# The stage ahead of the exponentials: two token buffers, key tiles ahead of query tiles, scores over 51 rows, fewer clearings, waits by chunk

## The chip, the cores and the metric

The kernel runs on one core of one Trainium2 chip. The metric is the device time of one execution in microseconds (us). Of the kernel before there are three timed runs and one profiled execution. Engines are named as in the profile: PE (TensorE matmul), PEld (TensorE weight load), DVE (VectorE), ACT (ScalarE), POOL (GpSimd), SP (SyncE, which issues nearly all DMAs).

## The reference, cut to what matters

Four samples of 2048 tokens with 256 features pass an adaptive layer norm, a differential attention and a ternary linear layer:

```python
h = _layernorm(x) * (1 + ca) + sa
q, k = h @ Wq.T, h @ Wk.T                 # 32 score heads of 8 features
v = h @ Wv.T                              # 16 value heads of 16 features
scores = (q * 8 ** -0.5) @ k.T            # 2048 x 2048 for each score head
attn_w = softmax(scores)                  # float32
aw = attn_w[:, :, 0] - lam * attn_w[:, :, 1]
attn = rmsnorm(aw @ v) * subln_w * (1 - LAMBDA_INIT)
x = x + ga * (attn @ Wo.T)
h = _layernorm(x) * (1 + cb) + sb
x = x + gb * (h @ (ternary(weight) * scale).T)
```

## The kernel before, in words

A sample (B = 4) has NC = 4 chunks of CH = 512 tokens, and a chunk has 4 blocks of 128 tokens. The program has two parts.

**The first part** works on sample 0 alone, chunk by chunk (`tc`), before any exponential. For one chunk:

- SP loads 512 tokens (512 KB) into `a_x` (`a_load`).
- DVE takes mean and variance (`a_stats`), POOL raises the variance to the power -1/2 (`a_power`), DVE writes `normed` (`a_apply`, L1103).
- PE transposes `normed` (`turn`, L831, 64 PE instructions), ACT copies the result to `p_hT` with the modulation's scale and bias (`turned`, L760).
- PE projects four tiles of 128 features: 0 and 1 are the queries, 2 and 3 the keys (L845, 64 instructions for two tiles), then the values (L837, 64 instructions). The order on PE is: projections of `tc`, `turn(tc + 1)`, values of `tc`.
- ACT copies each tile out of PSUM to `a_qk` (`projected`, L770 and L772) and its bf16 head to `p_parts` (L776). POOL subtracts (`rest`, L707), ACT rounds again (`middle`, L781), POOL subtracts again (`low`, L713). A float32 number thus becomes three bf16 parts. `p_parts` has two buffers, one of which lies in `probs`.
- DVE takes signs and absolute maxima of query tiles (L1146, L1147) and maximum and minimum of key tiles (L1148, L1149) in `first_bounds`, and copies the values to `a_v` (`first_values`, L1165).
- SP stores the parts to scratch in DRAM (`store_qk`, L447, three DMAs for one tile) and the values (`store_v`, L451), and reads back what group 0 needs (`first_rows`, L486 and L493, five DMAs; it waits until the chunk's parts and values have landed).

After the last chunk an upper bound of each query's scores is formed from the extremes of all keys. DVE builds `box_w` (`m_means`), PE multiplies it with the signed queries in six steps (`m_step`, L895), DVE reduces these (`m_evacuate`, L1310 and L1311), splits the result in three bf16 parts (`maxima_split`, L1327 to L1331), PE transposes them (L882), ACT copies them to `m_parts` (L797), and SP writes them from there into three rows of `queries[0]` (`first_maxima`, L518, four DMAs of 2048 tokens). The keys have ones in the same three rows (written by `clear(keys[i], ONE_PAIR)`), so that the score product subtracts the bound by itself.

**The second part** is the attention. `queries` and `keys` hold two halves, at rows 0 and 64. A half has KQ = 48 rows of products of parts and 3 rows of maxima. A score product reads KS_ROWS = 64 rows of a half; the 13 rows that remain are zero in `queries` (cleared by POOL at the start). For 128 keys and 512 queries of one pair, PE makes two score products (`scores`, L915), ACT takes one exponential over 1024 columns (L810), and PE multiplies with the values (`weighted`, L932). Two exponentials make a unit; a body has 128 units and the program 16 bodies. Pieces of the next sample's first part and of the last sample's output part lie between the units by a written table (`steps_of`). PE waits for all loads of a group (`group_loaded`, `loads_of`) before the first unit of that group. SP, PE and DVE wait for `m_flag`, which says whether the bound is too loose; in the profiled execution the branch behind it is not taken.

The order on each engine is that of the code; no planner or scheduler is at work. Waits are on counting semaphores.

## Time and profile before

| | us |
|---|---|
| median of 3 runs | 3849.46 |
| lowest and highest | 3845.53, 3850.63 |
| profiled execution, its own time | 3844.91 |
| profiled execution, span | 3843.2 |

| engine | busy us | share of the span |
|---|---|---|
| PE | 3685.4 | 96% |
| ACT | 3712.2 | 97% |
| DVE | 2149.8 | 56% |
| POOL | 623.0 | 16% |

The busy time of an engine is a mean over two parts with different limits. In the first of 40 slices of the span (96 us each) ACT is busy for 3 tenths, in each of the 38 slices that follow for 9 tenths or more, and in the last for 4. A busy PE is not PE at its peak, since ends of matmuls are modelled. The granted clock of PE is a mean over a stretch of two levels, 1.2 GHz (0.50) and 2.4 GHz (1.00).

### The profile page before, as it was taken

What the parts mean: (1) busy time and instruction counts of PE and PEld (TensorE: products, weight loads), DVE (VectorE), ACT (ScalarE), POOL (GpSimd) and SP (SyncE); (2) the same over time, 40 slices, a digit from 0 to 9 for tenths busy, and PEclk for the clock granted to TensorE, in tenths of its full rate; (3) what the DMA queues carried; (4) which work ended last, traced back from release to release, by engine and by line L of the source; (5) the groups of instructions that cost most, each with busy time, mean ns of one, the idle gap of its engine ahead of it and who ended that gap; (6) DMA issues with size and microseconds to landing.
All of it is one profiled execution on the core that took longest, in us unless ns stands there. A gap on an engine that the chain in (4) does not pass through costs nothing.

```text
span 3843.2 us, 76108 instructions
## 1 busy us (share of the span) xinstructions
PE 3685.4 (96%) x32110; PEld 933.9 (24%) x32110; DVE 2149.8 (56%) x3654; ACT 3712.2 (97%) x4067; POOL 623.0 (16%) x402
## 2 busy tenths in 40 slices
PE   7999999999999999999999999999999999999997
PEld 5222222122222222222222222222222222211122
DVE  7556656463366666665347566666435566555233
ACT  3999999999999999999999999999999999999994
POOL 5111212112121211212112121211211111010010
PEclk8999999999999999999999999999999999999998
DMA  7221121212212221131121212221112111201101
GB/s 242 53 67 26 47 43 39 50 34 56 49 42 48 59 53 42 47 68 39 46 53 52 57 36 48 61 51 43 46 35 51 31 42 31 46 4 25 37 20 41
DMA packets 132420, 188.33 MB, mean 49 GB/s; under 512 B 11100, under 2 KB 107100, under 8 KB 132064
## 3 DMA queue, kind: packets, MB, share of 16 engines
q1 hardware_dynamic: 131248, 182.53, 19.3%
q8 instruction: 257, 4.21, 0.5%
q14 instruction: 99, 0.81, 0.1%
q10 hardware_dynamic: 816, 0.79, 0.1%
HBM read 97.61 MB, written 85.47 MB: 48 GB/s over the span
## 4 chain that ended last, share of the span: by engine, by line
ACT 54%; PE 29%; issue 13%; DVE 2%; SPq 1%; POOL 0%; DMA 0%; DVEq 0%; ACTq 0%; POOLq 0%
ACT probs L810 52%; PE ps L932 15%; PE ps L915 10%; PE ps L837 2%; ACT wmod_sb L810 2%; DVE seg_t L1255 1%; PE ps L845 1%; PE ps L831 1%; DVE normed L1103 0%; SPq L447 0%; PE ps L895 0%; DMA v_scr<-a_v 0%; SPq L486 0%; DMA a_x<-in_x_dram 0%; DVE e_tmp L1207 0%
## 5 line engine op out<-in xcount | busy, mean ns | idle before, releaser
L810 ACT ACTIVATE probs<-ps 128x1024 f32<-128x1024 f32 x3894 | 3584.0, 1206 | 22.1 <-PE ps L915 21.2
L932 PE MATMUL ps<-probs,values 128*32 128x512 f32 x15576 | 2077.1, 605 | 7.7 <-DVE seg_t L1255 3.0
L915 PE MATMUL ps<-queries,keys 64*128 64x512 bf16 x8192 | 1395.6, 385 | 89.5 <-DMA queries<-wmod_sb 7.0
L915 PEld LDWEIGHTS ps<-queries,keys 64*128 64x128 bf16 x8192 | 347.3, 93 | 1727.8 <-ACT probs L810 1560.8
L743 POOL TENSOR_TENSOR seg_rs<-seg_ms,neg_half 64x16 f32<-64x16 f32 x128 | 370.2, 2892 | 2372.7 <-DVE seg_ms L1264 2372.7
L1255 DVE STREAM_TRANSPOSE seg_t<-ps 128x512 f32<-128x512 f32 x128 | 91.8, 717 | 1001.2 <-PE ps L932 1001.2
L932 PEld LDWEIGHTS ps<-probs,values 128*32 128x32 f32 x15576 | 306.9, 108 | 593.8 <-issue 489.9
L1243 DVE SCALAR_TENSOR_TENSOR wmod_sb<-wmod_sb,d_y 128x1024 f32<-128x1024 f32 x303 | 371.1, 1225 | 10.4
L1229 DVE TENSOR_SCALAR d_y<-ps 128x1024 f32<-128x1024 f32 x101 | 123.7, 1225 | 124.3 <-PE ps L915 124.3
L810 ACT ACTIVATE wmod_sb<-ps 128x1024 f32<-128x1024 f32 x101 | 129.8, 1285 | 0.0
L831 PE MATMUL ps<-ident,normed 128*32 128x128 f32 x2048 | 103.8, 295 | 25.7 <-DVE normed L1103 25.7
L1244 DVE SCALAR_TENSOR_TENSOR wmod_sb<-wmod_sb,gates 128x1024 f32<-128x1024 f32 x101 | 123.7, 1225 | 3.5
L1241 DVE SCALAR_TENSOR_TENSOR wmod_sb<-d_y 128x1024 f32<-128x1024 f32 x101 | 123.1, 1219 | 0.0
L1239 DVE TENSOR_TENSOR d_y<-d_y,gates 128x1024 f32<-128x1024 f32 x101 | 119.7, 1185 | 0.8
L1273 DVE SCALAR_TENSOR_TENSOR seg_a<-seg_n,subln_sb 32x256 f32<-32x256 f32 x256 | 109.3, 427 | 6.0
L1207 DVE TENSOR_TENSOR e_tmp<-ps,e_gate 128x512 f32<-128x512 f32 x64 | 44.2, 691 | 120.3 <-PE ps L837 120.3
L831 PEld LDWEIGHTS ps<-ident,normed 128*32 128x32 f32 x2048 | 71.5, 120 | 153.2 <-issue 138.2
L932 PE MATMUL ps<-wmod_sb,values 128*32 128x512 f32 x808 | 107.6, 605 | 0.0
L683 POOL CAST a_parts<-a_qk 128x512 bf16<-128x512 f32 x48 | 29.4, 613 | 411.8 <-DVE wmod_sb L1244 396.8
L1269 DVE TENSOR_TENSOR seg_n<-seg_d,seg_rs 64x256 f32<-64x256 f32 x128 | 54.6, 426 | 68.0 <-POOL seg_rs L743 64.5
L1277 DVE STREAM_TRANSPOSE seg_o<-seg_a 32x512 f32<-32x512 f32 x128 | 89.6, 700 | 4.4
L837 PE MATMUL ps<-w_f,e_hT 128*32 128x256 f32 x1024 | 80.0, 397 | 8.3 <-DVE e_hT L1204 6.6
(153 smaller groups left out, 1733.6 us busy)
## 6 DMA issues: line engine op xcount, KB each, us to landing
queries<-q_scr SPq DMA_DIRECT2D x62, 384.0 KB
keys<-k_scr SPq DMA_DIRECT2D x62, 384.0 KB
v_scr<-a_v SPq DMA_DIRECT2D x16, 1024.0 KB, 4.5
values<-v_scr SPq DMA_DIRECT2D x31, 512.0 KB
q_scr<-a_parts SPq DMA_DIRECT2D x28, 384.0 KB, 2.6
k_scr<-a_parts SPq DMA_DIRECT2D x28, 384.0 KB, 2.6
a_x<-in_x_dram SPq DMA_DIRECT2D x16, 512.0 KB, 12.8
attn_scr<-seg_o SPq DMA_DIRECT2D x128, 64.0 KB, 1.7
```

The costliest lines, as they stand in the source:

```text
L743: nc.gpsimd.tensor_tensor(seg_rs[:, :], seg_ms[:, :], neg_half[0:64, :], ALU.pow).then_inc(seg_rs_done, 1)
L810: nc.scalar.activation(probs_of(unit)[:, n % PAIRS, :, :], slots[slot_of(body, n)], ACT.Exp).then_inc(exp_done, 1)
L831: last = nc.tensor.matmul(bank[j:j + 32, n * P:(n + 1) * P], src[:, n, c * P + j:c * P + j + 32], ident[:, :], start=True, stop=True)
L837: last = nc.tensor.matmul(bank[j:j + 32, (n % 2) * E:(n % 2 + 1) * E], hT[:, c, n * P + j:n * P + j + 32], w[:, c, :], start=(c == 0), sto ...
L915: last = nc.tensor.matmul(slots[slot_of(body, n)][:, half, :], keys[buf][at:at + KS_ROWS, n % PAIRS, blk * P:(blk + 1) * P], queries[buf][ ...
L932: last = nc.tensor.matmul(pv[j:j + VW, :], values[buf][:, blk, half, :], probs_of(unit)[:, pair, half, :], start=(blk == 0), stop=(blk == ...
L1229: V.tensor_scalar(d_y[:, :], slots[n % SLOTS].rearrange("p h c -> p (h c)"), EXP_LOW, QUARTER_LOG2E, ALU.max, ALU.mult).then_inc(d_read, 1)
L1239: link.then(V.tensor_tensor(d_y[:, :], d_y[:, :], d_n, ALU.subtract))
L1241: link.then(V.scalar_tensor_tensor(d_out, d_y[:, :], POLY[4], d_y[:, :], ALU.add, ALU.mult))
L1243: link.then(V.scalar_tensor_tensor(d_out, d_out, POLY[i], d_y[:, :], ALU.add, ALU.mult))
L1244: V.scalar_tensor_tensor(d_out, d_out, POLY[0], d_n, ALU.add, ALU.mult).then_inc(d_done, 1)
L1255: V.transpose(seg_t[:, :, :].rearrange("p c d -> p (c d)"), pv).then_inc(pv_read, 1)
```

## The change

The second part is as before, except for the number of rows that a score product reads and for two waits. The diff, cut to its core:

```diff
-    KS_ROWS = 64
+    KS_ROWS = KQ + PARTS
+    FIRST_TILES = (2, 3, 0, 1)
+    FIRST_BANKS = (0, 1, 4, 5, 2, 3, 4)
...
+        p_x = (a_x, e_x)
...
+            def p_load(tc):
+                sp.dma_start(p_x[tc % 2][:, :, :], x[0:1, tc * CH:(tc + 1) * CH, :].rearrange("o (n p) e -> p (o n) e", p=P)).then_inc(p_x_loaded[tc % 2], DMA)
...
-                rows_of(0, 0, 0, group_loaded[0], slice(tc * CH, (tc + 1) * CH))
+                rows_of(0, 0, 0, p_rows_loaded[tc], slice(tc * CH, (tc + 1) * CH))
...
-            def first_maxima():
+            def first_maxima(loaded, t=slice(0, T)):
...
-            sp.wait_ge(a_normed, 1)
-            a_load(0, 1)
-            sp.wait_ge(consts_set, 8)
             for tc in range(NC):
...
+                if tc < NC - 1:
+                    sp.wait_ge(a_normed, tc + 1)
+                    if tc + 2 < NC:
+                        p_load(tc + 2)
+                    else:
+                        a_load(1, 0)
+                for p, i in enumerate(FIRST_TILES):
+                    sp.wait_ge(a_split, (tc + 1) * 4 + p + 1)
                     store_qk(p_parts[tc % 2], 0, tc, i, p_stored[tc % 2])
...
+            sp.wait_ge(p_maxima, 1)
+            first_maxima(p_maxima_loaded[0], slice(0, CH))
             first_rows(NC - 1)
-            sp.wait_ge(p_maxima, NC)
-            first_maxima()
+            for tc in range(1, NC):
+                sp.wait_ge(p_maxima, tc + 1)
+                first_maxima(p_maxima_loaded[tc], slice(tc * CH, (tc + 1) * CH))
...
             nc.gpsimd.memset(neg_half[:, :], -0.5).then_inc(consts_set, 1)
+            clear(keys[0], ONE_PAIR)
...
-            clear(keys[0], ONE_PAIR)
-            clear(queries[0], 0.0)
...
             a_power(0)
-            clear(keys[1], ONE_PAIR)
-            clear(queries[1], 0.0)
+            pool.wait_ge(a_normed, 1)
             nc.gpsimd.memset(a_v[:, :, :, :, :], 0.0).then_inc(consts_set, 1)
...
+            a_power(1)
+            clear(keys[1], ONE_PAIR)
...
+            def valued(tc):                      # on ACT; first_values, its like on DVE, is removed
+                if tc == 0:
+                    act.wait_ge(consts_set, 5)
+                else:
+                    act.wait_ge(p_v_stored, tc * DMA)
+                for j in range(2):
+                    act.wait_ge(p_valued, tc * 2 + j + 1)
+                    for n in range(2):
+                        last = nc.scalar.activation(a_v[:, :, 2 * j + n, :, 0:VD], ps[:, 6 + j, n * E:(n + 1) * E].rearrange("p (g h d) -> p g h d", g=NG, h=2), ACT.Copy)
+                    last.then_inc(p_valued_read, 1)
...
             for i in range(M_BOUNDS):
-                m_step(0, i, ps[:, i, :])
+                if i == NC:
+                    pe.wait_ge(p_bounded, NC * 4)
+                m_step(0, i, ps[:, FIRST_BANKS[i], :])
...
+                        if body == 0 and u < NB and u % BPC == 0:
+                            pe.wait_ge(p_rows_loaded[u // BPC], CHUNK_LOADS * DMA)
+                        if body == 0 and u < UNITS and u % NB == 0:
+                            pe.wait_ge(p_maxima_loaded[u // NB], 4 * DMA)
```

Also changed: the tokens of chunk `tc` are read from `p_x[tc % 2]`; the tiles are projected, copied, split, bounded and stored in the order 2, 3, 0, 1; DVE runs `m_means` once it has bounded the two key tiles of the last chunk, and its two query tiles after that; one half of `late_product` on PE (`gate_rows`) stands behind the transposes of the maxima; ACT waits before its first exponential until the last chunk's parts, which lie in `probs`, are stored.

On POOL, the start of the program. Before:

```order
L661 AFFINE_SELECT head_mask<-head_mask 128x16 [waits ident_set]
L666 MEMSET keys 128x2048
L666 MEMSET queries 128x2048
L674 TENSOR_TENSOR a_rstd<-a_ve,neg_half 128x4 [waits a_var,consts_set]
L666 MEMSET keys 128x2048
L666 MEMSET queries 128x2048
L696 MEMSET a_v 128x2048
L698 MEMSET a_v 128x64 [waits consts_set]
L699 MEMSET ones 128x128
L674 TENSOR_TENSOR a_rstd<-a_ve,neg_half 128x4 [waits a_var]
```

Now:

```order
L689 AFFINE_SELECT head_mask<-head_mask 128x16 [waits ident_set]
L696 TENSOR_TENSOR a_rstd<-a_ve,neg_half 128x4 [waits a_var,consts_set]
L718 MEMSET a_v 128x2048 [waits a_normed]
L720 MEMSET a_v 128x64 [waits consts_set]
L721 MEMSET ones 128x128
L696 TENSOR_TENSOR a_rstd<-a_ve,neg_half 128x4 [waits a_var]
L673 MEMSET keys 128x2048
```

Both clearings of `queries` are gone, that of `keys[0]` stands ahead of these rows, and the large memsets behind the first power now wait for the first `normed`.

On SP, the end of the first part, from the stores of the last chunk's second pair of tiles. Before:

```order
L447 DMA k_scr<-probs 128x3x512 [waits a_split]
L447 DMA k_scr<-probs 128x2x512
L447 DMA k_scr<-probs 128x512
L451 DMA v_scr<-a_v 128x8x256 [waits p_valued_read]
L486 DMA queries<-q_scr 48x2x512 [waits p_v_stored,p_stored1]
L486 DMA keys<-k_scr 48x2x512
L486 DMA queries<-q_scr 48x2x512
L486 DMA keys<-k_scr 48x2x512
L493 DMA values<-v_scr 128x256
L518 DMA queries<-wmod_sb 3x2048 [waits p_maxima]
L518 DMA queries<-wmod_sb 3x2048 x3
```

Now:

```order
L458 DMA q_scr<-probs 128x3x512 [waits a_split]
L458 DMA q_scr<-probs 128x2x512
L458 DMA q_scr<-probs 128x512
L462 DMA v_scr<-a_v 128x8x256 [waits p_valued_read]
L529 DMA queries<-wmod_sb 3x512 [waits p_maxima]
L529 DMA queries<-wmod_sb 3x512 x3
L497 DMA queries<-q_scr 48x2x512 [waits p_v_stored,p_stored1]
L497 DMA keys<-k_scr 48x2x512
L497 DMA queries<-q_scr 48x2x512
L497 DMA keys<-k_scr 48x2x512
L504 DMA values<-v_scr 128x256
L529 DMA queries<-wmod_sb 3x512 [waits p_maxima]
```

The maxima of chunk 0 (four small DMAs) stand ahead of the wait for the stored values and of the last five row loads; two more groups of four follow the last row shown.

On DVE, the last chunk. Before:

```order
L1148 TENSOR_REDUCE box<-a_qk 128x1 [waits p_projected_read]
L1149 TENSOR_REDUCE box<-a_qk 128x1
L1284 TENSOR_REDUCE m_mean<-a_sum 128x2 [waits ident_set,p_bounded]
L1286 TENSOR_SCALAR box<-m_mean 128x2 [waits m_chain]
L1286 TENSOR_SCALAR box<-m_mean 128x2
L1290 TENSOR_TENSOR box_w<-head_mask,box 128x80 [waits m_chain]
L1290 TENSOR_TENSOR box_w<-head_mask,box 128x80 x3
L1165 COPY a_v<-ps 128x8x2x16 [waits p_valued,p_v_stored]
L1165 COPY a_v<-ps 128x8x2x16
L1165 COPY a_v<-ps 128x8x2x16 [waits p_valued]
L1165 COPY a_v<-ps 128x8x2x16
L1298 TENSOR_REDUCE m_size<-box 128x2 x2
```

Now:

```order
L1204 TENSOR_REDUCE box<-a_qk 128x1 [waits p_projected_read]
L1205 TENSOR_REDUCE box<-a_qk 128x1
L1328 TENSOR_REDUCE m_mean<-a_sum 128x2 [waits ident_set,p_bounded]
L1330 TENSOR_SCALAR box<-m_mean 128x2 [waits m_chain]
L1330 TENSOR_SCALAR box<-m_mean 128x2
L1334 TENSOR_TENSOR box_w<-head_mask,box 128x80 [waits m_chain]
L1334 TENSOR_TENSOR box_w<-head_mask,box 128x80 x3
L1202 TENSOR_SCALAR q_sign<-a_qk 128x512 [waits p_projected_read]
L1202 TENSOR_SCALAR q_sign<-a_qk 128x512
L1203 TENSOR_REDUCE a_qabs<-a_qk 128x1
L1202 TENSOR_SCALAR q_sign<-a_qk 128x512 [waits p_projected_read]
L1202 TENSOR_SCALAR q_sign<-a_qk 128x512
```

The four copies of the values are gone from DVE, and the work on the two query tiles comes behind `m_means` where it came before it.

## Rows read from the trace of the kernel before

**Rows 1.** Page, part 5: line, engine, op, tiles, count, busy, mean ns, idle before.
```profile
L810 ACT ACTIVATE probs<-ps 128x1024 f32<-128x1024 f32 x3894 | 3584.0, 1206 | 22.1 <-PE ps L915 21.2
```
**Rows 2.** Timeline 0 to 21: start, length, engine, line, op, tiles, count, idle before.
```profile
8.34 3.58 PE L820 MATMUL ps<-silu,wmod_sb 128*128 128x4 f32 x16 [8.34 <-DMA wmod_sb<-in_wmod_dram]
...
10.05 1.80 POOL L666 MEMSET keys<- 128x2048 f32 x1
10.13 6.40 DVE L1103 TENSOR_SCALAR normed<-a_x,moments,a_rstd 128x256 f32<-128x256 f32 x4 [1.21 <-POOL a_rstd L674]
...
16.68 3.64 PE L831 MATMUL ps<-ident,normed 128*32 128x128 f32 x64 [4.76 <-DVE normed L1103]
```
**Rows 3.** Timeline 95 to 125: the normalisation with POOL idle.
```profile
103.11 1.38 DVE L1103 TENSOR_SCALAR normed<-a_x,moments,a_rstd 128x256 f32<-128x256 f32 x4 [1.28 <-POOL a_rstd L674]
```
**Rows 4.** Waits until 130 us: who waited for whom, in total, times, longest.
```profile
PE ps L831 <- DVE normed L1103: 15.8, 3, 6.8
...
DVE stats L1092 <- DMA a_x<-in_x_dram: 10.5, 3, 4.5
```
**Rows 5.** Timeline of PE, the chunks' starts.
```profile
21.30 3.66 PE L845 MATMUL ps<-a_hT,w_q 128*32 128x256 f32 x64 [0.98 <-ACT a_hT L760]
...
28.20 1.96 PE L831 MATMUL ps<-ident,normed 128*32 128x128 f32 x64
...
33.40 3.66 PE L845 MATMUL ps<-e_hT,w_q 128*32 128x256 f32 x64
...
47.36 3.64 PE L831 MATMUL ps<-ident,normed 128*32 128x128 f32 x64 [6.84 <-DVE normed L1103]
```
**Rows 6.** Timeline 60 to 95: the last chunk, PE, DVE and SP.
```profile
65.07 4.71 SPq L447 DMA_DIRECT2D q_scr<-a_parts  x6
...
73.65 3.63 PE L845 MATMUL ps<-e_hT,w_q 128*32 128x256 f32 x64
...
77.96 1.08 SPq L451 DMA_DIRECT2D v_scr<-a_v  x1
...
82.88 0.16 DVE L1284 TENSOR_REDUCE m_mean<-a_sum 128x2 f32<-128x8 f32 x1
...
87.04 1.40 DVE L1165 COPY a_v<-ps 128x256 f32<-128x256 f32 x4
```
**Rows 7.** Timeline 95 to 125: from the split maxima to the first score.
```profile
97.94 1.46 PE L882 MATMUL ps<-ident_bf,m_split 128*96 128x128 bf16 x16
...
98.63 2.05 ACT L797 ACTIVATE wmod_sb<-ps 96x512 bf16<-96x512 f32 x4 [12.98 <-PE ps L882]
...
106.34 1.46 PE L915 MATMUL ps<-queries,keys 64*128 64x512 bf16 x6 [6.95 <-DMA queries<-wmod_sb]
...
106.99 7.44 ACT L810 ACTIVATE probs<-ps 128x1024 f32<-128x1024 f32 x8 [6.31 <-PE ps L915]
```
**Rows 8.** Chain of waits, 80 to 130: start, length, what.
```profile
93.77 5.84 DMA v_scr<-a_v
...
101.96 0.83 SPq L518
...
104.23 2.06 DMA queries<-wmod_sb
```
**Rows 9.** Timeline 16 to 60: SP's first store, POOL's last part of chunk 0.
```profile
28.88 4.14 SPq L447 DMA_DIRECT2D q_scr<-a_parts  x6
...
33.80 1.17 POOL L713 TENSOR_TENSOR a_parts<-e_tmp,a_parts 128x512 bf16<-128x512 f32 x1
```
**Rows 10.** Windows: stretch, length, busy (instructions) of each engine, clock, DMA share, GB/s.
```profile
33.40:40.50 7.10, 7.10 (x132) 4.88 (x124) 2.58 (x8) 2.45 (x4) 1.57 (x2) 1.00 1.03 318
...
77.20:80.50 3.30, 3.30 (x68) 1.83 (x64) 2.53 (x6) 3.08 (x7) 2.80 (x3) 1.00 1.09 383
```
**Rows 11.** Timeline 95 to 125: one unit of PE, score products and weighted products.
```profile
117.96 0.60 PE L915 MATMUL ps<-queries,keys 64*128 64x512 bf16 x4
118.49 1.06 PE L932 MATMUL ps<-probs,values 128*32 128x512 f32 x8
```

More of the change, by code:

```diff
@@ L210, in loads_of @@
             return (body + 1) * GROUP_LOADS
-        return sum(FIRST_LOADS if k == 0 else TURN_LOADS if k % GP == 0 else GROUP_LOADS for k in range(body + 1))
+        return sum(TURN_LOADS if k % GP == 0 else GROUP_LOADS for k in range(1, body + 1))
     ROW_LOADS = 2 * 2
@@ L366, in adaln_diff_attention @@
         p_maxima = sem("p_maxima")
+        p_x_loaded = [sem(f"p_x_loaded{i}") for i in range(2)]
+        p_rows_loaded = [sem(f"p_rows_loaded{i}") for i in range(NC)]
+        p_maxima_loaded = [sem(f"p_maxima_loaded{i}") for i in range(NC)]
         ident_set = sem("ident_set")
@@ L517, in first_maxima @@
                         head = half * 2 + s
-                        sp.dma_start(queries[0][at:at + PARTS, s, :], m_parts[head * PARTS:(head + 1) * PARTS, :]).then_inc(group_loaded[0], DMA)
+                        sp.dma_start(queries[0][at:at + PARTS, s, t], m_parts[head * PARTS:(head + 1) * PARTS, t]).then_inc(loaded, DMA)
             def m_store(b, stored):
@@ L525, in _ @@
             sp.dma_start(c_sb[:, :, :], cT.rearrange("(c p) b -> p c b", p=P)).then_inc(c_loaded, DMA)
-            a_load(0, 0)
-            for first, over, loaded in ((0, 2 * E, wmod_loaded), (2 * E, 6 * E, wmod_rest_loaded)):
-                sp.dma_start(wmod_sb[:, :, first:over], wmod[:, first:over].rearrange("(c p) f -> p c f", p=P)).then_inc(loaded, DMA)
+            p_load(0)
+            sp.dma_start(wmod_sb[:, :, 0:2 * E], wmod[:, 0:2 * E].rearrange("(c p) f -> p c f", p=P)).then_inc(wmod_loaded, DMA)
+            p_load(1)
+            sp.dma_start(wmod_sb[:, :, 2 * E:6 * E], wmod[:, 2 * E:6 * E].rearrange("(c p) f -> p c f", p=P)).then_inc(wmod_rest_loaded, DMA)
             for w, src in ((wf, wfT), (wo, woT)):
@@ L565, in _ @@
                     runs = sp.snap(exact_runs, min_val=0, max_val=B - 1)
-                    sp.wait_ge(group_loaded[0], loads_of(0, b * GP) * DMA)
+                    if b > 0:
+                        sp.wait_ge(group_loaded[0], loads_of(0, b * GP) * DMA)
+                    else:
+                        for tc in range(NC):
+                            sp.wait_ge(p_rows_loaded[tc], CHUNK_LOADS * DMA)
+                            sp.wait_ge(p_maxima_loaded[tc], 4 * DMA)
                     with sp.Fori(0, NG) as g:
@@ L662, in _ @@
                                     pattern=[[HD, NS // EC]], channel_multiplier=-1).then_inc(ident_set, 1)
[L664 to L670 removed]
+            pool.wait_ge(consts_set, 2)
             def a_power(job):
@@ L785, in _ @@
                 projected(tc, 0)
-                for i in range(1, 4):
-                    projected(tc, i)
-                    middle(tc, i - 1)
+                for p in range(1, 4):
+                    projected(tc, p)
+                    middle(tc, p - 1)
                 if tc < NC - 1:
@@ L797, in _ @@
                 nc.scalar.activation(m_parts[:, k * CH:(k + 1) * CH], ps[0:PARTS * NS, k, :], ACT.Copy).then_inc(p_maxima, 1)
+            act.wait_ge(p_stored[1], 2 * (4 * len(ROW_RUNS) * DMA))
             for body in range(B * GP):
@@ L949, in _ @@
                 pe.wait_ge(p_turned_read, (tc + 1) * EC)
-                for i in range(4):
+                for j, i in enumerate(FIRST_TILES):
                     if tc > 0:
-                        pe.wait_ge(p_projected_read, (tc - 1) * 4 + i + 1)
+                        pe.wait_ge(p_projected_read, (tc - 1) * 4 + j + 1)
                     for p in range(PIECES):
@@ L1149, in bounds, with first_bounds @@
                 return V.tensor_reduce(box[:, c, 1, at], src, axis=AX.X, op=ALU.min)
-            def first_bounds(tc, i):
-                dve.wait_ge(p_projected_read, tc * 4 + i + 1)
-                bounds(i, tc).then_inc(p_bounded, 1)
-            def first_values(tc):
-                if tc == 0:
-                    dve.wait_ge(consts_set, 8)
-                else:
-                    dve.wait_ge(p_v_stored, tc * DMA)
-                for j in range(2):
-                    dve.wait_ge(p_valued, tc * 2 + j + 1)
-                    for n in range(2):
-                        last = V.tensor_copy(a_v[:, :, 2 * j + n, :, 0:VD], ps[:, 6 + j, n * E:(n + 1) * E].rearrange("p (g h d) -> p g h d", g=NG, h=2))
-                    last.then_inc(p_valued_read, 1)
+            def first_bounds(tc, p):
+                dve.wait_ge(p_projected_read, tc * 4 + p + 1)
+                bounds(FIRST_TILES[p], tc).then_inc(p_bounded, 1)
             def a_bounds(job, i, tc):
@@ L1340, in _ @@
                     a_apply(tc + 1)
-                for i in range(1, 4):
-                    first_bounds(tc, i)
+                first_bounds(tc, 1)
                 if tc == NC - 1:
-                    dve.wait_ge(p_bounded, NC * 4)
+                    dve.wait_ge(p_bounded, (NC - 1) * 4 + 2)
                     dve.wait_ge(ident_set, 6)
                     mlink = m_means(0)
-                first_values(tc)
+                first_bounds(tc, 2)
+                first_bounds(tc, 3)
                 if tc == 1:
```

99 lines of the change are left out of this document (53 added, 46 removed).

## The prediction

> **What bounds the kernel now.** Three views, in this order. First the groups of the page: the 3894 exponentials keep ACT busy for 3584.0 us and cost it 22.1 us of idle time in all [rows 1]; that is 0.92 us each, with nearly no hole. So from its first exponential on, the program is as long as ACT's work, and the first part is simply time ahead of it: the first exponential starts at 106.99 [rows 7]. Whatever brings that start forward is taken off the end one for one, as long as nothing later runs dry. Second the waits of the first part: PE waits for `normed` three times, 15.8 us in all, and DVE waits for tokens three times, 10.5 us [rows 4]. Third the chain of waits: it runs through SP, through the last store of values (5.84 us to land) and through the issue of the maxima to the first score [rows 8]. So the first part is held by a relay of loads, DVE, PE, the split and SP's stores. I follow each piece of it and ask what is late next.
>
> **The start.** The first `normed` takes 6.40 us while POOL clears `keys[1]`, `queries[1]` and `a_v` [rows 2]; the same four instructions take 1.38 us where POOL is idle [rows 3]. The large memsets now wait for `normed`, so it ends at 10.13 + 1.38 = 11.5. PE is still on its first products until 8.34 + 3.58 = 11.9 [rows 2], which becomes the bound: the first transposes start at about 12.0 in place of 16.68, and the first projection at 16.6 in place of 21.30 [rows 5]. That is -4.7 us. The clearing of `keys[0]` ahead of the identity (1.80 us, as the one in rows 2) lies in the time in which nothing has landed yet; if that cover failed it would cost those 1.80. The load of the second chunk stands behind the first part of `wmod`, which the first product waits for, and so delays nothing on this path.
>
> **The period of a chunk.** From the start of the projections of chunk 0 to those of chunk 1 PE needs 33.40 - 21.30 = 12.1 us with no wait [rows 5]. Until the projections of chunk 3, at 73.65 [rows 6], three periods took 52.35 us, or 17.45 each. The 16 us above 3 x 12.1 are mostly the later waits for `normed`, 15.8 - 4.76 = 11.0 [rows 2, 4], and transposes that take 3.64 us after such a wait where they take 1.96 without one [rows 5], twice 1.7. The waits come from the loads, issued by SP only after `normed` and behind other DMAs; with two buffers chunks 2 and 3 are loaded more than one period ahead, so all of the wait for tokens goes. What is late next? POOL has eight subtractions of 1.17 us or a little more [rows 9] and one power, under 11 us. ACT takes over four copies of values. The trace does not show them on ACT; DVE takes 1.40 us for the four [rows 6], and ACT took 2.05 us for four copies of twice the columns [rows 7], so between 1 and 2 us, and I take 1.8. They stand behind the last `middle` and ahead of the next chunk's first tile, where ACT would otherwise wait for PE, so I cost them at 0 to 1 us a period. DVE loses the same copies. With small waits from one engine to the next I take 13.0 us for a period, between PE's 12.1 and SP's 14 (below). The projections of chunk 3 then start at 16.6 + 39.0 = 55.6.
>
> **From the last projections to the split.** Before, 97.94 - 73.65 = 24.3 us [rows 6, 7]. `m_means` started 9.2 us after the projections [rows 6]. It now needs two tiles rather than four: half of PE's work, 3.6 us less, less a part for the waits between tiles: -3.2. The bounds of two query tiles (some 1.4 us each) come behind it: +2.8. The value copies, 1.40 us between `m_means` and the sizes [rows 6], are gone: -1.4. The products of the first twelve blocks no longer wait for all bounds, but DVE reads them only after those, so that earns nothing. Sum -1.8, giving 22.5: split ready at 78.1.
>
> **From the split to the first score.** Before, 106.34 - 97.94 = 8.4 us. Now PE and ACT hand over the first 512 maxima after 98.63 - 97.94 + 0.6 = 1.3 us [rows 7]; SP then issues four DMAs, the last of them 104.23 - 101.96 = 2.3 us after the first, and that one lands 2.06 us later [rows 8]. 5.7 us in all, -2.7, since five row loads and the wait for the values no longer stand ahead. The first score would come at 83.8.
>
> **SP and the transfers.** SP's first store was at 28.88 [rows 9] and comes at 24.2. It then waits for chunk 1's first tile, one period later, at 36.3. A chunk takes SP from 65.07 to 79.04, that is 14.0 us [rows 6], more than the 13.0 above. So from 36.3 on SP falls behind and does not wait: 36.3 + 3 x 14.0 = 78.3, with the last store of values issued at about 77.6 and landed at 83.4 (5.84 us, rows 8). A chunk moves 3.1 MB of parts (four tiles of 128 x 6 x 512 bf16), 1 MB of values, 0.5 MB of rows and 0.5 MB of tokens; 15.3 MB at 318 to 383 GB/s [rows 10] take 40 to 48 us, from 36.3 to 76 to 84. SP, transfers and the engines' chain thus end within about a microsecond of each other.
>
> The maxima are issued right behind the last store of values. The Trainium skill, "DMA: Bandwidth & Descriptors", section Queues, rings and completion order, says that a DMA's semaphore rises only after all earlier writes of that DMA engine. By it the first score could not come ahead of the values' landing, 83.4 plus a little; without it, 83.8 stands. No row here shows small DMAs behind a large store, so the rule is not tested.
>
> Three sums that meet at 83 to 84 are each without slips; I take 85.0 for the first score and 85.65 for the first exponential (0.65 later, rows 7), against 106.99: **-21.3 us**. ACT's new wait for the parts in `probs` is covered, as these are issued ahead of the values. Row loads of chunk 3 come some 3 us after the first score and are needed at unit 12, 12 x 1.84 = 22 us after it. Those of group 1 waited for the gates, which move with the rest, and are needed 64 units after the start.
>
> **51 rows.** The row count of a product is not in the trace except as 64. From below: shorter products earn nothing, since ACT is the bound. From above: if two halves could no longer run side by side, a unit's four products would take 1.20 us instead of 0.60 [rows 11]. I take zero, the nearest row being the 64-row one. The Trainium skill, "TensorE: Matmul & The Clock Gate", section LDWEIGHTS, counts a weight load by its columns and not by its rows, which would make it zero too.
>
> The sum for the profiled execution is 3844.91 - 21.3 = 3823.6. The median of the runs lies 4.55 above that execution, so for a median: 3849.46 - 21.3 = **3828**.
>
> **Rivals.**
> 1. The transfers bound the first part. For it: the stores become one dense stream, and a store of 1 KB packets may not hold 318 GB/s beside loads. At 300 GB/s a chunk takes 17 us: 36.3 + 51 + 5.84 = 93.1 for the first score, -13: 3836. Against it: 383 GB/s was reached with stores and row loads mixed [rows 10].
> 2. The change does not do what it says: the wait for tokens goes, but DVE and POOL block each other (a `normed` of 6.40 against 1.38) and the period stays at 17.45. Then only the start, the last chunk and the maxima count: -4.7 - 1.8 - 2.7 = -9.2: 3840. Against it: the first period had both engines at work and took 12.1.
> 3. Slower: products over 51 rows cost PE more. A unit takes PE 0.60 + 1.06 = 1.66 us [rows 11] and ACT 2 x 0.92 = 1.84, so PE has 0.18 us, 45 ns for each of four products. From 45 ns PE becomes the bound, and with 2048 units 48 ns a product already eats the gain. At 90 ns: 2048 x 0.18 = +369, less 21: about 4197. With the halves one after the other: 2048 x 0.42 = +860. For it: 51 is no multiple of 32, and all products in the trace have 64 or 128 rows. Against it: nothing in the order or number of instructions changes.
>
> **How the numbers follow.** Forecast 76%, with periods from 12.1 to 14.6: -26 to -17, and medians of the runs that may fall some us to either side, 3819 to 3834. Rival 1: 14%, rival 2: 5%, rival 3: 5%. The range 3818 to 3840 holds the forecast and the first two, less their tails. A measurement of this kernel tells 0.2% (7.7 us) from no change. Faster by more: the forecast, rival 1 and most of 2, less a little for slips: 0.92. Within it: 0.04. Slower: 0.04.
>
> **What would show it.** In the profile after: `normed` of chunk 0 in about 1.4 us and transposes at 12; no DVE wait for tokens after the first; projections 12 to 14 us apart, chunk 3's at 53 to 58; DVE's `m_mean` about 6 us behind them; SP without a wait from about 36 on; the first exponential at 81 to 90; after it ACT's idle time still about 22 us in all, and 0.60 us for four score products. Wrong would be a first exponential after 94, projections 17 us apart, or ACT waiting for score products in every unit.

## The result, and the profile after

| | before | after |
|---|---|---|
| median of the runs (range, runs), us | 3846.99 (3844.92 to 3850.63, 5) | 3827.73 (3825.29 to 3829.82, 5) |
| profiled execution: time, span, us | 3844.91, 3843.2 | 3828.01, 3826.3 |
| first exponential starts, us | 106.99 | 90.77 |
| last exponential ends, us | 3796.46 | 3781.71 |

The ratio is 0.9949, with the interval 0.9936 to 0.9962: 0.5% faster. The medians differ by 19.3 us; the two profiled executions differ by 16.9 us, and the arguments below go by these. 16.2 of the 16.9 lie ahead of the first exponential. From there to the last, before took 3689.47 us and after 3690.94, and what is left behind it shrank from 46.7 to 44.6 us. 3828 was forecast with a first exponential at 85.65: it comes 5.1 us later than that, and the forecast's base, 3849.46, was itself above the median of before that the later runs gave. That the median hit the forecast is luck: the profiled execution took 3828.01 where 3823.6 was forecast, 4.4 too long, and the median after lay 0.3 below that execution, where the forecast had added 4.55, taken from three runs of before. The two slips, +4.4 and -4.8, cancel. The forecast step from before to after, 21.3 us, came out as 16.9 in the profiled executions, and as 16.4 between the medians when the same kernel was run again (e9, 3844.42 to 3828.01).

The page after, two groups of part 5, answers to [rows 1, 11]:

```profile
L852 ACT ACTIVATE probs<-ps 128x1024 f32<-128x1024 f32 x3894 | 3583.8, 1204 | 23.4 <-PE ps L957 22.7
...
L957 PE MATMUL ps<-queries,keys 51*128 51x512 bf16 x8192 | 1395.9, 385 | 86.9 <-DMA queries<-wmod_sb 4.2
```

The exponentials are as many and as long as in [rows 1], with 1.3 us more idle time. The product over 51 rows takes 385 ns on average. So nearly the whole change lies in the first 91 us, and the timeline of that part, engine by engine, tells it (start, length, engine, line, operation, tiles, count, idle time before):

```profile
9.73 1.38 DVE L1156 TENSOR_SCALAR normed<-a_x,moments,a_rstd 128x256 f32<-128x256 f32 x4 [1.21 <-POOL a_rstd L696]
11.17 1.80 POOL L718 MEMSET a_v<- 128x2048 f32 x1 [1.48 <-DVE normed L1156]
...
16.69 5.84 PE L887 MATMUL ps<-a_hT,w_k 128*32 128x256 f32 x64 [0.99 <-ACT a_hT L786]
...
31.00 3.64 PE L887 MATMUL ps<-e_hT,w_k 128*32 128x256 f32 x64
...
57.72 3.64 PE L887 MATMUL ps<-e_hT,w_k 128*32 128x256 f32 x64
...
63.46 0.16 DVE L1328 TENSOR_REDUCE m_mean<-a_sum 128x2 f32<-128x8 f32 x1
...
67.60 1.72 DVE L1202 TENSOR_SCALAR q_sign<-a_qk 128x512 bf16<-128x512 f32 x2
69.84 2.07 DVE L1202 TENSOR_SCALAR q_sign<-a_qk 128x512 bf16<-128x512 f32 x2
...
82.09 1.94 PE L924 MATMUL ps<-ident_bf,m_split 128*96 128x128 bf16 x16
...
84.42 0.68 SPq L462 DMA_DIRECT2D v_scr<-a_v  x1
85.14 3.76 SPq L529 DMA_DIRECT2D queries<-wmod_sb  x4
...
90.77 7.44 ACT L852 ACTIVATE probs<-ps 128x1024 f32<-128x1024 f32 x8 [5.93 <-PE ps L957]
```

`normed` takes 1.38 us, where it took 6.40 [rows 2], and the memset of `a_v` now starts only behind it. Chunk 3's projections start 41.0 us after those of chunk 0, where before they came 52.4 later [rows 5, 6]; the three distances are 14.3, 12.1 and 14.6. The last row is the one that was at 106.99 [rows 7]. Two rows catch the eye: the first pair of projections takes 5.84 us where 3.66 was the rule [rows 5], and between the split (82.09) and SP's issue of the maxima (85.14) lie 3.05 us.

The waits until 92 us, of the pairs that [rows 4] shows:

```profile
DVE stats L1145 <- DMA a_x<-in_x_dram: 1.5, 1, 1.5
...
PE ps L873 <- DVE normed L1156: 0.6, 1, 0.6
```

10.5 us have become 1.5, and 15.8 have become 0.6. The chain of waits (start, length, what) no longer runs through the landing of the values, but through SP's own queue:

```profile
82.62 0.65 SPq L458
83.32 1.05 SPq L458
84.42 0.68 SPq L462
85.14 0.83 SPq L529
86.01 1.18 SPq L529
87.24 0.97 SPq L529
88.25 1.72 DMA queries<-wmod_sb
```

and two stretches of it, in the columns of [rows 10], show the transfers busy all the time (share 1.05 and 0.97):

```profile
40.00:60.00 20.00, 18.32 (x364) 11.35 (x358) 18.23 (x31) 13.65 (x29) 15.80 (x14) 1.00 1.05 329
60.00:80.00 20.00, 15.39 (x239) 11.44 (x229) 18.52 (x40) 8.28 (x20) 9.65 (x8) 0.81 0.97 311
```

### The profile page after: what moved, and what is told of

Same layout as the page of the kernel before. It is cut to its first block, busy times and chain, and to the rows that moved or that the text cites. A ratio compares the mean times of both kernels' runs of the same rounds, so it can differ in the third digit from the quotient of the medians.

```text
span 3826.3 us, 76125 instructions
## 1 busy us (share of the span) xinstructions
PE 3683.2 (96%) x32110; PEld 930.3 (24%) x32110; DVE 2138.4 (56%) x3638; ACT 3716.1 (97%) x4083; POOL 620.9 (16%) x400
## 3 DMA queue, kind: packets, MB, share of 16 engines
q1 hardware_dynamic: 131320, 182.53, 19.3%
q8 instruction: 257, 4.21, 0.5%
## 4 chain that ended last, share of the span: by engine, by line
ACT 54%; PE 30%; issue 13%; DVE 2%; SPq 1%; POOL 0%; DMA 0%; DVEq 0%; POOLq 0%; ACTq 0%
ACT probs L852 52%; PE ps L974 15%; PE ps L957 10%; PE ps L879 2%; ACT wmod_sb L852 2%; PE ps L887 1%; DVE seg_t L1299 1%; PE ps L873 1%; SPq L458 0%; PE ps L937 0%; DMA wmod_sb<-in_wmod_dram 0%; DVE e_tmp L1251 0%; POOL a_parts L739 0%; SPq L497 0%; PE ps L924 0%
## 5 line engine op out<-in xcount | busy, mean ns | idle before, releaser
L957 PE MATMUL ps<-queries,keys 51*128 51x512 bf16 x8192 | 1395.9, 385 | 86.9 <-DMA queries<-wmod_sb 4.2
L957 PEld LDWEIGHTS ps<-queries,keys 51*128 51x128 bf16 x8192 | 347.1, 93 | 1725.7 <-ACT probs L852 1555.9
L873 PE MATMUL ps<-ident,normed 128*32 128x128 f32 x2048 | 100.4, 287 | 10.8 <-DVE normed L1156 10.5
L705 POOL CAST a_parts<-a_qk 128x512 bf16<-128x512 f32 x48 | 29.4, 613 | 411.5 <-DVE wmod_sb L1288 396.5
L1321 DVE STREAM_TRANSPOSE seg_o<-seg_a 32x512 f32<-32x512 f32 x128 | 89.6, 700 | 4.4
L879 PE MATMUL ps<-w_o,e_attn 128*32 128x256 f32 x1024 | 79.3, 387 | 9.6 <-DVE e_x L1252 6.4
```

What stands on the lines that cost most here:

```text
L873: last = nc.tensor.matmul(bank[j:j + 32, n * P:(n + 1) * P], src[:, n, c * P + j:c * P + j + 32], ident[:, :], start=True, stop=True)
L879: last = nc.tensor.matmul(bank[j:j + 32, (n % 2) * E:(n % 2 + 1) * E], hT[:, c, n * P + j:n * P + j + 32], w[:, c, :], start=(c == 0), sto ...
L957: last = nc.tensor.matmul(slots[slot_of(body, n)][:, half, :], keys[buf][at:at + KS_ROWS, n % PAIRS, blk * P:(blk + 1) * P], queries[buf][ ...
```

## Experiments

The runs were to tell two things: whether the gain comes from the wait for tokens and the contention at the start, as forecast, or from the other parts (the order of tiles, the rows, the maxima); and whether the 5 us that are missing come from SP, which is still behind its stores when the maxima are ready, or from the engines ahead of the split. The recorded expectations use letters for their theories, and not the same ones throughout: up to e8, A is the relay of engines and B is SP with the transfers (B1: full transfers hold SP up, B2: its own issuing does); in e10, A is SP and B the split. Each kernel is the changed one with one edit. The first pair of projections takes 3.66 us in some profiled executions and 5.4 to 5.8 in others, so positions are compared from the start of chunk 1's projections on. "P1" is that start:

| kernel | median us (range, runs) | ratio to before | P1 | split | maxima issued | first exponential | P1 to it |
|---|---|---|---|---|---|---|---|
| changed | 3827.73 (3825.29-3829.82, 5) | 0.9949 | 31.00 | 82.09 | 85.14 | 90.77 | 59.8 |
| e1 one buffer | 3838.73 (3836.66-3842.04, 10) | 0.9982 | 30.68 | 95.17 | 96.48 | 101.47 | 70.8 |
| e2 clearings | 3832.21 (3830.28-3832.37, 5) | 0.9962 | 34.90 | 85.45 | 88.46 | 94.09 | 59.2 |
| e3 queries first | 3827.13 (3826.17-3829.83, 4) | 0.9952 | 28.86 | 79.67 | 82.85 | 88.79 | 59.9 |
| e4 maxima late | 3834.04 (3832.70-3835.44, 7) | 0.9970 | 28.77 | 79.37 | 90.57 | 95.71 | 66.9 |
| e5 64 rows | 3826.74 (3825.07-3828.25, 4) | 0.9951 | 28.75 | 79.27 | 82.97 | 88.79 | 60.0 |
| e6 rows of chunk 2 late | 3823.98 (3822.75-3824.74, 4) | 0.9944 | 30.65 | 81.14 | 82.46 | 87.50 | 56.9 |
| e7 few values | 3825.71 (3825.30-3827.71, 4) | 0.9950 | 28.31 | 82.04 | 83.36 | 88.39 | 60.1 |
| e8 values behind maxima | 3825.69 (3824.22-3827.58, 4) | 0.9950 | 28.70 | 79.42 | 80.74 | 85.52 | 56.8 |
| e9 changed, again | 3828.01 (3826.52-3829.20, 5) | 0.9957 | 30.60 | 81.17 | 84.47 | 90.13 | 59.5 |
| e10 as e6, again | 3823.06 (3821.99-3825.74, 5) | 0.9947 | 28.44 | 78.99 | 80.31 | 85.33 | 56.9 |

Before had medians of 3846.99 (changed), 3845.46 (e1 to e4), 3845.18 (e5 to e8) and 3844.42 (e9, e10) beside these runs, on different chips. The intervals of the ratios reach 0.0010 to 0.0017 to either side, that is 4 to 6.5 us. So only e1 is told from the changed kernel by its interval; e4, e2 and e10 (beside e9) differ by 6.3, 4.5 and 5 us with ranges that do not touch; everything smaller rests on the positions in one profiled execution each.

**e1: one buffer for the tokens.**

```
-        p_x = (a_x, e_x)
+        p_x = (a_x, a_x)
...
-            p_load(1)
...
+            sp.wait_ge(a_normed, 1)
+            p_load(1)
...
+                    if p == 1 and tc < NC - 1:
+                        sp.wait_ge(a_normed, tc + 2)
+                        if tc + 2 < NC:
+                            p_load(tc + 2)
```

> The changed kernel with one token buffer again: chunk 1 is loaded once chunk 0 is normalised, chunks 2 and 3 once the chunk ahead is normalised and behind the stores of the chunk's first two tiles and the row loads, as before the change. Theory A (a relay of engines: waits for tokens were most of what went): DVE waits for tokens again, 8 to 11 us in three waits, projections 15 to 17 us apart, first exponential at 98 to 102 in place of 90.8, time 8 to 11 us longer. Theory B (SP and the transfers end the first part, and the engines only need to keep up): the waits come back, but SP and the transfers catch up meanwhile, so the first exponential moves by 2 to 5 us only.

The time rises by 11 us, and the distance from P1 to the first exponential by 11.0. The waits that the change had removed are back:

```profile
DVE stats L1145 <- DMA a_x<-in_x_dram: 14.3, 4, 4.8
...
PE ps L873 <- DVE normed L1156: 11.0, 2, 6.1
```

This is the largest single part of the gain. On the engines it is larger than 11: from P1 to the projections of chunk 3 it took 40.1 us, as before (40.25), where the changed kernel has 26.7, and the split comes 13.4 us later after P1 (64.5 for 51.1). That is the 3 x 4.45 of the forecast. 2.4 us of it come back at the end: SP is idle when the later split arrives, issues the maxima 1.3 us behind it, and the first exponential starts 6.3 us after the split for 8.7. The edit brings back the one buffer and the old place of the loads in SP's queue together; the two were not told apart.

**e2: the clearings of the queries again, and the large memsets without their wait.** The clearing of `keys[0]` stays ahead of the identity.

```
+            clear(queries[0], 0.0)
...
-            pool.wait_ge(a_normed, 1)
+            clear(keys[1], ONE_PAIR)
+            clear(queries[1], 0.0)
             nc.gpsimd.memset(a_v[:, :, :, :, :], 0.0).then_inc(consts_set, 1)
```

> The changed kernel with the two clearings of the queries back and with the large memsets of POOL behind its first power again, without a wait for the first normalised tokens. Scores still read 51 rows. Theory A: the first normed takes about 6.4 us in place of 1.4, transposes start at 16.7 in place of 12.1, and all that follows moves by 4.6: first exponential at 95 to 96. Theory B says the same here, since the transfers cannot start before the first split tile. A slack between the start and the end of the first part would show as less than 3 us.

The timeline of its start shows the four instructions of `normed` beside three memsets:

```profile
9.69 1.80 POOL L673 MEMSET keys<- 128x2048 f32 x1
9.77 6.39 DVE L1157 TENSOR_SCALAR normed<-a_x,moments,a_rstd 128x256 f32<-128x256 f32 x4 [1.21 <-POOL a_rstd L697]
11.43 1.80 POOL L673 MEMSET queries<- 128x2048 f32 x1
13.17 1.80 POOL L720 MEMSET a_v<- 128x2048 f32 x1
...
16.31 3.64 PE L874 MATMUL ps<-ident,normed 128*32 128x128 f32 x64 [4.21 <-DVE normed L1157]
```

6.39 us again, and PE waits 4.21 for it. The time rises by 4.5, the first exponential by 3.3. P1 moves from 31.00 to 34.90, and the rest of the first part is not longer: a plain delay of the start, as both theories had it.

**e3: queries ahead of keys.**

```
-    FIRST_TILES = (2, 3, 0, 1)
+    FIRST_TILES = (0, 1, 2, 3)
...
                 first_bounds(tc, 1)
+                first_bounds(tc, 2)
+                first_bounds(tc, 3)
                 if tc == NC - 1:
-                    dve.wait_ge(p_bounded, (NC - 1) * 4 + 2)
+                    dve.wait_ge(p_bounded, NC * 4)
```

> The changed kernel with tiles in the order 0, 1, 2, 3 again (queries first), and the means of the keys formed after all four tiles of the last chunk. Theory A as in the prediction (keys first earn 0.4 us net on DVE): first exponential up to 1 us later. Theory C (the work on the last two query tiles, 4.9 us in the trace after and not 2.8, stands alone behind the means, so keys first cost more than they give): from the last projections to the split 1 to 2 us less than the 24.3 us in the changed kernel. Theory B: whatever the split does, the maxima wait for SP, so the first exponential moves by less than 1 us.

No difference, in the time or from P1 on (59.9 against 59.8). But that is no proof that the order is free, for two other waits cover it. SP issues the maxima 3.2 us after the split here too. And PE does not take the split when DVE has it:

```profile
73.70 3.58 PE L862 MATMUL ps<-silu,wmod_sb 128*128 128x4 f32 x16 [0.76 <-ACT a_v L819]
...
77.26 1.02 DVE L1375 TENSOR_TENSOR m_split<-w_low,m_split 128x512 bf16<-128x512 f32 x1
...
77.87 1.87 PE L1021 MATMUL ps<-wmod_sb,silu 128*4 128x256 f32 x4
79.67 1.82 PE L924 MATMUL ps<-ident_bf,m_split 128*96 128x128 bf16 x16
```

DVE is done at 78.28, 49.4 us after P1, where e4, e5 and e10 take 50.5; PE comes 1.4 us later, since products of the modulation stand ahead of the transposes. These waited for ACT's copies of the values (L819), and the copies for the last value store to land (5.7 us). So on DVE alone keys first cost about 1 us and did not earn the forecast's 0.4, which is the direction of the third theory; but the split itself came no sooner (25.0 us after the last projections, 24.6 in e4, e5 and e10), and the time does not show it.

**e4: maxima loaded together, behind the rows.**

```
-            sp.wait_ge(p_maxima, 1)
-            first_maxima(p_maxima_loaded[0], slice(0, CH))
             first_rows(NC - 1)
+            sp.wait_ge(p_maxima, NC)
+            first_maxima(p_maxima_loaded[0])
```

> The changed kernel with the maxima awaited and sent as a whole again: first the last chunk's five row loads (which wait for the stored values), then four DMAs of 2048 tokens each. Theory A: the wait for the values, 5.2 us, and 2.4 us of row loads stand ahead of the maxima again: first exponential 6.5 to 8 us later, 97 to 99. Rival: the maxima could not land ahead of the store of values in any case (they landed 0.4 us behind it in the changed kernel), so only the row loads and the longer DMAs count, 3 to 5 us.

The timeline of its SP and PE shows the queue that came back:

```profile
82.63 0.67 SPq L462 DMA_DIRECT2D v_scr<-a_v  x1
88.28 0.34 SPq L497 DMA_DIRECT2D queries<-q_scr  x1
...
90.57 2.91 SPq L529 DMA_DIRECT2D queries<-wmod_sb  x4
...
95.00 1.46 PE L954 MATMUL ps<-queries,keys 51*128 51x512 bf16 x6 [12.93 <-DMA queries<-wmod_sb]
```

SP waits for the values until 88.28, issues five row loads, and only then the maxima: 15.6 us from the split (79.37) to the first score, and a time 6.3 us longer. By the distance from P1 it is 7.1 us, within the 6.5 to 8 of the first theory and above the 3 to 5 of the rival. So the edit earns 6 to 7 us in the changed kernel. It did not earn that against before, whose 8.4 us from split to score were already about as short as the 8.0 of after: there the values landed 1.7 us after the split (99.6 and 97.94). What it does is to keep the queue from turning into the new bound once everything else had moved forward.

**e5: products over 64 rows.**

```
-    KS_ROWS = KQ + PARTS
+    KS_ROWS = 64
...
             clear(keys[0], ONE_PAIR)
+            clear(queries[0], 0.0)
...
             clear(keys[1], ONE_PAIR)
+            clear(queries[1], 0.0)
```

> The changed kernel with score products over 64 rows again; the 13 extra rows are cleared, queries[0] at the start of the program and queries[1] behind the second power, both in time in which POOL would wait. If the row count costs or earns nothing: 0.60 us for four products with a rival of 0.60 at 51 rows, the same 1.84 us per unit, and a time within 2 us of the changed kernel's. If 51 rows earned something in the second part (its idle time of ACT, for one): 3 us or more slower here.

```profile
L959 PE MATMUL ps<-queries,keys 64*128 64x512 bf16 x8192 | 1395.3, 385 | 89.3 <-DMA queries<-wmod_sb 6.3
```

8192 products take 1395.3 us over 64 rows and 1395.9 over 51. The medians lie 1 us apart. The row count is free in both directions, as far as these runs can tell.

**e6 and e10: chunk 2's rows behind the first maxima.**

```
-                    if p == 1 and tc > 0:
+                    if p == 1 and 0 < tc < NC - 1:
                         first_rows(tc - 1)
             first_maxima(p_maxima_loaded[0], slice(0, CH))
+            first_rows(NC - 2)
             first_rows(NC - 1)
```

> The changed kernel with the third chunk's five row loads moved behind the first chunk's maxima; they are needed 8 units after the first score. Theory B (at the end of the first part the maxima wait for SP, which is held up by full transfer queues): SP reaches the maxima 3 us earlier, so they are issued as soon as they are there; first exponential 1.5 to 3 us earlier, measured from the start of chunk 1's projections (59.8 us in the changed kernel). Theory A (the engines' relay ends last): no change, under 0.5 us.

> Chunk 2's rows of keys and queries loaded after the first maxima instead of before the last chunk's stores, as in e6. Theory A (SyncE's queue, behind its stores, is what the first score waits for): 3 us less than the changed kernel on the same chip, 3824 to 3825 us, the first score 5 to 6 us after the split. Theory B (the split is what bounds, and e6 fell low by scatter): within 1 us of the changed kernel, 3827 us.

> The changed kernel once more, beside the version of e6 on the same chip. Both theories expect 3827.5 us (3826 to 3829), and 59 to 61 us from the start of chunk 1's projections to the first exp, with 8 us of it between the split and the first score. The start of chunk 1's projections is expected at 28.5 to 31 us, as it has scattered until now.

In e10 SP has issued the last values at 78.43 and is idle when the split comes:

```profile
78.43 0.70 SPq L462 DMA_DIRECT2D v_scr<-a_v  x1
78.99 1.94 PE L925 MATMUL ps<-ident_bf,m_split 128*96 128x128 bf16 x16
80.31 3.28 SPq L529 DMA_DIRECT2D queries<-wmod_sb  x4
...
84.85 0.82 PE L958 MATMUL ps<-queries,keys 51*128 51x512 bf16 x6 [2.11 <-DMA queries<-wmod_sb]
```

The changed kernel beside it on the same chip:

```profile
81.17 1.94 PE L924 MATMUL ps<-ident_bf,m_split 128*96 128x128 bf16 x16
...
83.75 0.67 SPq L462 DMA_DIRECT2D v_scr<-a_v  x1
84.47 3.78 SPq L529 DMA_DIRECT2D queries<-wmod_sb  x4
...
89.42 1.46 PE L957 MATMUL ps<-queries,keys 51*128 51x512 bf16 x6 [4.51 <-DMA queries<-wmod_sb]
```

5.9 us from split to score against 8.3. The time is 3823.06 against 3828.01, and the ranges of the five runs each do not touch; e6 had 3823.98. That is the best version of the study, 4 to 5 us below the changed kernel. The two profiled executions lie 6.0 us apart (3828.01 and 3821.99). Of these the moved loads explain 2.6 (P1 to first exponential, 59.5 to 56.9); 2.2 lie in P1, which scatters, and are no merit of the edit; 1.2 lie behind the first exponential. e6 had a late P1 (30.65) and a time as low, so the medians may hold more than the 2.6 that the profiles explain; that part is open.

**e7: most values stored later.** For the first sample, head groups 1 to 7 are given the last chunk's values four times, so that part of the output isn't the reference's; the work on PE, ACT and DVE is the same.

```
-                store_v(0, tc, p_v_stored)
+                store_v_some(tc, slice(0, 1))
...
+            for tc in range(NC):
+                store_v_some(tc, slice(1, NG))
```

> The changed kernel, but each chunk's store of values ahead of the first score moves only group 0's values (128 KB in place of 1 MB); the other seven groups are stored behind the maxima, so that for sample 0 they hold the last chunk's values. The number of DMAs that SP issues ahead of the first score is the same, the bytes are 3.7 MB fewer of about 20. Theory B1 (the transfers hold SP up): SP's chunk takes about 13.5 us in place of 15.5, the maxima are issued as soon as they are ready and land in about 2 us; first exponential 3 to 4 us earlier. Theory B2 (SP's own issue time holds it up): SP's chunk stays at 15.5 and the first exponential moves by less than 1 us. Theory A: less than 0.5 us.

A mixed result. SP's chunk becomes shorter, with value stores issued at 48.27, 62.28 and 77.16 where the changed kernel has them at 52.16, 68.79 and 84.42; the maxima are issued at once, 1.3 us after the split, and the first score is 5.9 us behind it. But chunk 3's projections start 29.4 us after P1, where it is 26.7 in the changed kernel and 25.8 to 26.1 in the others with two buffers, with one wait of PE for `normed`, 3.2 us, whose four instructions took 4.79 us beside POOL's subtractions. That hid the gain. The transfers, with a share of 0.90 and 0.83 in the two stretches, were no longer full. As many issues with fewer bytes took SP 15.0, 14.0 and 14.9 us a chunk for 16.0, 16.6 and 15.6: so the full transfers do hold SP up, though the 13.5 that were expected were not reached. The engines were not faster for it, so nothing here shows that the transfers bound them.

**e8: last values behind the maxima.** e6's edit, and the last chunk's values stored behind the first maxima and chunk 2's rows (the two buffers for parts change places, so that ACT's exponentials don't wait for the last parts).

```
+                if tc < NC - 1:
+                    sp.wait_ge(p_valued_read, 2 * (tc + 1))
+                    store_v(0, tc, p_v_stored)
...
             first_maxima(p_maxima_loaded[0], slice(0, CH))
+            first_rows(NC - 2)
+            sp.wait_ge(p_valued_read, 2 * NC)
+            store_v(0, NC - 1, p_v_stored)
             first_rows(NC - 1)
```

> A version meant to be faster: the two buffers of parts are swapped, so that the last chunk's parts lie in a_parts and the third's in probs, and the third chunk's row loads and the last chunk's store of values come behind the first chunk's maxima. Theory B1: with 1.5 MB less ahead of them the maxima are issued as soon as they are ready; first exponential 3 to 4 us earlier than in the changed kernel by the same distance (56 to 57 us from the start of chunk 1's projections in place of 59.8), time 3 to 4 us less. Theory A: no change. A risk: the last row loads, needed at unit 12, land some 10 us after the first score, which unit 12 (22 us) still covers.

From P1 on it is as fast as e6 and e10 (56.8 us) and not faster. With no value store ahead of them the first score comes 4.1 us after the issue of the first maxima, with one ahead 4.5 (e6, e10), and in the changed kernel 4.9. The chains of waits tell where that lies. From SP's issue of the last of the four to its landing it is 1.71 us in e8, 1.71 in e10, 1.72 in e6 and 1.72 in the changed kernel. From the first issue to the last it is 2.27, 2.64, 2.44 and 3.11. So the values in flight cost the maxima no landing time here; what differs is the time that SP takes to issue them, and a little the time from landing to score (0.19 us in e10, 0.39 in e6, 0.09 in the other two). Its median is above e10's, though the ranges overlap, and I draw nothing from that.

## Why the prediction was right, step by step

**The bound** was read rightly. The exponentials took the same 3584 us, and what was gained ahead of them (16.2) is the gain in span (16.9) within 0.7.

**The start**, -4.7 forecast: projections at 16.69 for 16.6. Right in size and cause, as e2 shows: 6.39 us for `normed` beside the memsets, 1.38 without them.

**The period**, 3 x 13.0 forecast: 41.03 us measured, of which 2.2 are the slow first pair, which no row had announced; 3 x 12.95 are left. That these fit 13.0 so well is in part luck: they are twice PE's bare 12.1 and once 14.6, with a hole of 1.12 us in PE's products and a wait of 0.56 for `normed` (the hole is shown in the last section), and not three small waits. e1 shows that it was the wait for tokens: 13.4 us on the engines, 11 in the time. The four value copies on ACT take 1.2 us, between the 1 and 2 of the forecast.

**The last projections to the split**, 22.5 forecast, 24.4 measured. `m_means` starts 5.7 us behind the projections (6 forecast), and the copies are gone. The mis-sized term is the bounds of the two query tiles: +2.8 in the sum, 4.9 measured (67.60 to 72.5). I had taken one tile at 1.4 us from a place where POOL was idle or nearly so. Here POOL works beside it:

```profile
67.72 1.31 POOL L732 TENSOR_TENSOR e_tmp<-a_qk,probs 128x512 f32<-128x512 f32 x1
69.00 1.34 POOL L739 TENSOR_TENSOR probs<-a_rest,probs 128x512 bf16<-128x512 f32 x1
70.30 1.33 POOL L739 TENSOR_TENSOR probs<-e_tmp,probs 128x512 bf16<-128x512 f32 x1
```

and two `q_sign` take 1.72 or 2.07 us, where they had taken 0.76 and 0.83 in the last chunk of before. Rows of before with the same company were there: two `q_sign` took 2.69, 2.67 and 1.71 us in its first three chunks. It is the contention that the first term was about, forgotten in the third. So this stretch, forecast 1.8 us shorter, is as long as before (24.3).

**The split to the first score**, 5.7 forecast, 8.0 measured: this step failed in the changed kernel. Its parts were right, since e6, e7 and e10 show 5.9 with SP free; but SP was not free. It issued its first maxima 3.05 us after the split where 1.3 were forecast, as two more stores and the values still stood ahead of them, and the four issues with their landing took 4.9 in place of 4.4. The cause is the term **SP and the transfers**: 14.0 us a chunk forecast, 16.0, 16.6 and 15.6 measured (value stores at 36.17, 52.16, 68.79, 84.42). SP also started late: its first store came at 27.01 for 24.2, that of chunk 1 at 38.59 for 36.3 (which was 24.2 + 12.1, PE's bare period, and not the 13.0 taken above). So its last value store was issued at 84.42 for 77.6, 2.3 us for the late start and 4.5 for the longer chunks. One store takes SP 0.43 us where the transfers have room (64.17 in the chain below, a share of 0.56 from 63.5 to 65.2) and mostly 1.1 to 1.3 where they are full (1.04 from 69.5 to 74):

```profile
64.17 0.43 SPq L458
...
70.24 1.34 SPq L458
71.62 1.29 SPq L458
72.96 1.26 SPq L458
```

**Rival 1** was thus right in a part. The transfers did take 16 of the 17 us a chunk that it named, at 311 to 329 GB/s. It did not decide the time, because only SP's last issues hang on them: they cost the first score 1.7 us for the wait behind the stores (3.05 less the 1.3 of the hand-over) and 0.8 for the slower issues. The 383 GB/s held against this rival are no row for stores and row loads mixed, as it says: stores fill that stretch (77.20 to 80.50), and the last row load had been issued at 71.99. **Rival 2** is out: periods of 12.1 to 14.6 us, not 17.45. **Rival 3** is out: 0.60 us for four products and 385 ns each, over 51 rows and over 64. The 8192 weight loads took 347.1 us over 51 rows, 347.3 over 64 in the kernel before. The rule of the Trainium skill that was weighed ("TensorE: Matmul & The Clock Gate", section LDWEIGHTS: a load is counted by columns) agrees with that.

The rule of the Trainium skill on completion order ("DMA: Bandwidth & Descriptors", section Queues, rings and completion order) is not refuted, and cost nothing here: in the changed kernel the values landed at about 89.6 and the last maxima at 89.97, in the order that it asks for, and these landed as fast after their issue (1.72 us) as in e8 with no values ahead of them (1.71). The 0.8 us by which e8 is quicker from first issue to score are SP's issue time.

**The sum**: 83.8 for the engines' chain, +2.2 for the first pair, +2.1 for the query bounds (with -0.2 of small change), +2.3 for SP, gives 90.2; the first score came at 90.06. The 1.2 us added for slips were less than a fifth of what slips came to. Step by step, against before (the forecast's own 1.2 for slips apart):

| step | forecast | measured |
|---|---|---|
| start | -4.70 | -4.61 |
| three periods | -13.35 | -11.32 |
| last projections to split | -1.80 | +0.08 |
| split to first score | -2.70 | -0.43 |
| sum | -22.55 | -16.28 |

The two large terms, with their causes, were right; the two small ones brought next to nothing. (The -26 at the good end of the forecast's span is also 1 us more than its terms give: 21.3 + 2.7 + 1.2 = 25.2.)

## What to carry to other kernels

When the parts of a serial opening are shortened together, the queue that only carried them becomes the last to end: ask of each issue in it whether the next wait needs it, and put those that nobody needs yet (here chunk 2's rows, needed only at unit 8, 8 x 1.84 = 15 us after the start) behind the one that is awaited. A duration read where the neighbouring engine is idle is no price for a step that moves to where that engine works; read it from a row with the same company. And where the gain of an edit is measured by undoing it, it can be far larger (e4: 6 us) than what it gave over the kernel before (0.4 from split to score), because the other edits have moved the bound onto it. An edit undone without effect (e3) may likewise be covered by a wait elsewhere: look at when the engine itself was done before calling it free.

## What the runs showed that I had not expected

**The first pair of projections.** 64 products take 3.66 us in six of the eleven profiled executions of changed kernels (e3, e4, e5, e7, e8, e10) and 5.43 to 5.84 in five (changed, e1, e2, e6, e9), and it is not the kernel's text: e6 and e10 are the same kernel with 5.50 and 3.66. The granted clock was 1.00 in both. The weight loads of the slow one come in fours with a hole that nothing in the profile explains:

```profile
17.09 0.23 PEld L887 LDWEIGHTS ps<-a_hT,w_k 128*32 128x32 f32 x4 [0.20 <-issue]
```

and in the other without one:

```profile
16.31 3.21 PEld L888 LDWEIGHTS ps<-a_hT,w_k 128*32 128x32 f32 x64 [1.24 <-issue]
```

Ten such holes of 0.20 us make nearly all of the 2.2. What makes them is open; no run here was aimed at it. It moves everything behind it, and so the first exponential.

**A hole in chunk 2's projections.** In nine of the eleven PE stops for 1.1 to 1.5 us after twelve products of chunk 2; in e1 and e7 it does not.

```profile
43.11 1.05 PE L887 MATMUL ps<-a_hT,w_k 128*32 128x256 f32 x12
45.27 3.00 PE L887 MATMUL ps<-a_hT,w_k 128*32 128x256 f32 x50 [1.12 <-issue]
```

The share of the transfers in the 3 us from the start of these projections was 1.08 in the changed kernel and 1.09 in e10, 0.91 in e7 and 0.86 in e1. That goes with full transfers, but no run was made to show it, and the cause is open.

**The issue time of SP** rises with how full the transfers are: the first four loads of maxima take it 2.91 us with a share of 0.02 (e8), 0.01 (e7) and 0.36 (e4), 3.28 with 0.81 (e10), and 3.76 with 1.01 (changed).
